# Pixel-major rows of the deformable-convolution stage by DMA transposes in a ring of four, and a reordered head

## The chip, the core and the metric

One core of one Trainium2 chip. The metric is the device time of one execution in microseconds (us), lower is better. TensorE writes only to PSUM; ScalarE (ACT), VectorE (DVE) and GpSimd (POOL) do the elementwise work; SyncE (SP) issues every DMA of this kernel, and the core's 16 DMA engines carry them out.

## What is computed

Two layers on `x` of shape (4, 128, 64, 64), f32. The first is group norm, a 1x1 convolution to q, k, v, attention over all 4096 pixels of an image, a projection and a residual. The second is the part that the change touches:

```python
out = relu(batchnorm(conv2d(x, w1), g1, b1))                 # h1
offsets = conv2d(out, w_off) + b_off                         # 18 channels
out = batchnorm(deform_conv(out, offsets, w2), g2, b2)       # samples h1 at 9 shifted points per pixel
return relu(out + x)

# deform_conv, in short
px = clip(row + tap_x + offset_x, 0, Hp - 1)                 # py likewise
xo = g_lt*xf[x0,y0] + g_rb*xf[x1,y1] + g_lb*xf[x0,y1] + g_rt*xf[x1,y0]
out = conv(xo, w, stride 3)
```

## The kernel before

Every f32 operand of a large matmul is split in two f16 halves, a high one and a low one, and a product is three matmuls (hi x hi, lo x hi, hi x lo). Engines run their own instruction streams, tied by semaphores: `after(engine, key, n)` waits until the n-th event of a kind; `stored(engine, sem, n)` waits for the n-th DMA on a semaphore. GpSimd first raises all semaphores by a constant (`OPEN`, L386 to L390) so that negative counts can be waited for, and the other engines wait for that (`s_open`).

Head (0 to 20 us). SyncE loads the first weights, the first image in four pieces (L272), the constants (L273) and the other weights (L274). VectorE scales the query weights, copies a product of weights from PSUM (L779) and makes the low halves of the weights (L783) once ScalarE has made the high ones (L559); then come the eight `gn_stats` of the image (L841), the group means over TensorE, and the affine of group norm on GpSimd (L401).

Then the attention of four images, which SyncE accompanies with 512 DMA transposes of probabilities (L290, 14 blocks of 128x128 f16 each), the first convolution of layer two, and its batch norm.

The offset stage (1699 to 1808 us) works on 32 bands of 8 image rows, 8 bands for each of 4 images. For band n: ScalarE makes h1 = relu(scale*y + bias) into one of four buffers `HT` (L699). TensorE turns it in four 128x128 pieces into PSUM (L1280). VectorE splits h1 into the padded halves `PDh`, `PDl` (L1024, L1026), which TensorE multiplies with the offset weights in 27 matmuls packed four to the array (L1290). The turned rows are pixel-major: ScalarE writes their high half (L656) and VectorE their low half (L1031) into `XS`, two buffers, and SyncE stores each band in four DMAs of 64 KB (L327) into the DRAM scratch `xt_dram`. The offsets themselves go from PSUM over `offset_rows` (L665), selection matmuls (L1298) and `offset_pixels` (L671) into `OFF`. The last image's stage also prepares the first hats on ScalarE (L679, L682). The order on ScalarE is: h1 of band n, rows of band n-2, offset rows of n-3, offset pixels of n-4. On VectorE it is: the split of band n, then the rows of band n-2.

After it, the sampling stage (1809 to 2323 us): SyncE loads windows of the stored rows (L345), queued behind all row stores; GpSimd makes interpolation weights (L524), TensorE turns them (L1311), samples (L1134 to L1136) and applies the second convolution.

The waits that order the offset stage on TensorE are few:

```python
after(pe, "hA", n + 1)            # h1 of this band
after(pe, "xe", n - 1)            # PSUM of the turned rows free
...                               # four pe.transpose, L1280
after(pe, "hp", b * NCH + min(rb + 2, NCH))
after(pe, "oe", n - 1)
...                               # 27 matmuls, L1290
```

## Time and profile before

| what | value |
|---|---|
| median of 3 runs | 2370.48 us (2368.9 to 2371.01) |
| the profiled execution's own time | 2370.24 us |
| its span | 2368.3 us |
| PE / DVE / ACT / POOL busy | 95% / 76% / 76% / 61% of the span |
| DMA queue q1 | 375.35 MB, 68.8% of 16 engines |
| mean granted TensorE clock | 0.984 |

The profile is one execution: its page gives busy shares, the span in 40 slices, the chain of work that ended last and the costliest groups; the trace behind it can be asked for single instructions. A wait is put down to the semaphore event that came last. In a timeline a row gives start, length, engine, line and operation, and in brackets the idle time ahead of it and what ended it.

### The profile page before, as it was taken

What the parts mean: (1) busy time and instruction counts of PE and PEld (TensorE: products, weight loads), DVE (VectorE), ACT (ScalarE), POOL (GpSimd) and SP (SyncE); (2) the same over time, 40 slices, a digit from 0 to 9 for tenths busy, and PEclk for the clock granted to TensorE, in tenths of its full rate; (3) what the DMA queues carried; (4) which work ended last, traced back from release to release, by engine and by line L of the source; (5) the groups of instructions that cost most, each with busy time, mean ns of one, the idle gap of its engine ahead of it and who ended that gap; (6) DMA issues with size and microseconds to landing.
All of it is one profiled execution on the core that took longest, in us unless ns stands there. A gap on an engine that the chain in (4) does not pass through costs nothing.

```text
span 2368.3 us, 73191 instructions
## 1 busy us (share of the span) xinstructions
PE 2260.2 (95%) x26668; PEld 1823.8 (77%) x26668; DVE 1808.2 (76%) x3885; ACT 1801.6 (76%) x2968; POOL 1448.9 (61%) x1103
## 2 busy tenths in 40 slices
PE   5999999999999999999999999969898999999994
PEld 3677777777777777777777777758666999999994
DVE  6778877777877777887777777758676887887887
ACT  5788888888888888888888888823376777776776
POOL 4569656666655666665666666675224666666661
PEclk9999999999999999999999999989999999999997
DMA  3878888879998888898787777786034444333447
GB/s 93 190 173 167 177 181 161 176 179 169 180 187 150 179 176 171 179 165 154 167 178 176 175 175 176 178 248 203 16 82 125 140 121 128 113 121 104 131 127 289
DMA packets 1048760, 377.63 MB, mean 159 GB/s; under 512 B 975490, under 2 KB 1035523, under 8 KB 1040387
## 3 DMA queue, kind: packets, MB, share of 16 engines
q1 hardware_dynamic: 1048578, 375.35, 68.8%
q8 instruction: 97, 1.59, 0.3%
q14 instruction: 85, 0.69, 0.1%
HBM read 98.69 MB, written 41.68 MB: 59 GB/s over the span
## 4 chain that ended last, share of the span: by engine, by line
PE 53%; POOL 24%; issue 16%; DVE 4%; DMA 2%; ACT 1%; POOLq 1%; SPq 0%; DVEq 0%; ACTq 0%
POOL interp L524 12%; POOL probs_split L416 10%; PE psum L1134 9%; PE psum L1135 9%; PE psum L1136 9%; PE psum L1174 7%; PE psum L1176 7%; PE psum L1175 7%; PE psum L1290 2%; DMA probsT_dma<-probs_split 2%; PE psum L1160 2%; PE psum L1298 1%; POOL col_hats L515 1%; POOL row_hats L510 1%; DVE neg_max L793 1%
## 5 line engine op out<-in xcount | busy, mean ns | idle before, releaser
L416 POOL TENSOR_TENSOR probs_split<-probs,probs_split 128x896 f16<-128x896 f32 x512 | 967.3, 1889 | 523.6 <-ACT probs_split L588 523.5
L793 DVE TENSOR_REDUCE neg_max<-psum 128x1 f32<-128x1024 f32 x512 | 626.4, 1223 | 307.6 <-PE psum L1136 305.3
L585 ACT ACTIVATE probs<-psum,exp_bias 128x1024 f32<-128x1024 f32 x512 | 570.5, 1114 | 184.6 <-DVE exp_bias L795 183.7
L1174 PE MATMUL psum<-vT_hi,probsT_dma 128*128 128x129 f16 x3584 | 637.6, 221 | 9.6 <-DMA probsT_dma<-probs_split 9.5
L1176 PE MATMUL psum<-vT_hi,probsT_dma 128*128 128x129 f16 x3584 | 637.3, 219 | 0.0
L1175 PE MATMUL psum<-vT_lo,probsT_dma 128*128 128x128 f16 x3584 | 637.1, 218 | 0.0
L588 ACT ACTIVATE probs_split<-probs 128x896 f16<-128x896 f32 x512 | 486.6, 950 | 23.1 <-ACT probs L585 1.0
L524 POOL TENSOR_TENSOR interp<-row_hats,col_hats 128x360 f32<-128x360 f32 x384 | 295.6, 798 | 185.4 <-PE psum L1311 174.4
L1134 PE MATMUL psum<-k_hi,q_hi 128*128 128x512 f16 x1024 | 388.5, 379 | 4.5 <-DVE q_lo L909 2.5
L1135 PE MATMUL psum<-k_lo,q_hi 128*128 128x512 f16 x1024 | 388.6, 379 | 0.0
L1136 PE MATMUL psum<-k_hi,q_lo 128*128 128x512 f16 x1024 | 388.6, 379 | 0.0
L1174 PEld LDWEIGHTS psum<-vT_hi,probsT_dma 128*128 128x128 f16 x3584 | 347.5, 97 | 11.2 <-DMA probsT_dma<-probs_split 10.9
L1175 PEld LDWEIGHTS psum<-vT_lo,probsT_dma 128*128 128x128 f16 x3584 | 352.8, 98 | 0.0
L1176 PEld LDWEIGHTS psum<-vT_hi,probsT_dma 128*128 128x128 f16 x3584 | 345.0, 96 | 0.0
L730 ACT ACTIVATE sampled_hi<-psum 128x432 f16<-128x432 f32 (+1 forms) x384 | 181.3, 497 | 81.3 <-PE psum L1136 81.2
L1063 DVE TENSOR_TENSOR sampled_lo<-psum,sampled_hi 128x432 f16<-128x432 f32 (+1 forms) x384 | 206.3, 554 | 47.1 <-ACT sampled_hi L730 42.5
L1055 DVE TENSOR_TENSOR interpT_lo<-psum,interpT_hi 120x384 f16<-120x384 f32 x384 | 190.4, 551 | 48.4 <-ACT interpT_hi L721 47.7
L1134 PE MATMUL psum<-sampled_hi,weights_hi 128*128 128x128 f16 x1152 | 214.4, 220 | 0.6 <-DVE sampled_lo L1063 0.6
L1136 PE MATMUL psum<-sampled_hi,weights_lo 128*128 128x128 f16 x1152 | 213.0, 219 | 0.0
L1135 PE MATMUL psum<-sampled_lo,weights_hi 128*128 128x128 f16 x1152 | 212.7, 219 | 0.0
L1134 PE MATMUL psum<-interpT_hi,xt_windows 120*128 120x144 f16 x1024 | 208.6, 227 | 2.1 <-DMA xt_windows<-xt_scratch 1.8
L721 ACT ACTIVATE interpT_hi<-psum 120x384 f16<-120x384 f32 x384 | 161.2, 492 | 64.9 <-PE psum L1311 54.2
(189 smaller groups left out, 4912.6 us busy)
## 6 DMA issues: line engine op xcount, KB each, us to landing
xt_windows<-xt_scratch SPq DMA_DIRECT2D x192, 320.0 KB
xt_scratch<-zeros_f SPq DMA_DIRECT2D x28, 576.0 KB, 4.3
probsT_dma<-probs_split SPq DMA_TRANSPOSE x512, 3.5
x_residual<-x SPq DMA_DIRECT2D x128, 64.0 KB, 2.4
x_scratch<-x_out SPq DMA_DIRECT2D x128, 64.0 KB, 2.1
x_rows<-x_scratch SPq DMA_DIRECT2D x32, 256.0 KB, 3.4
xt_scratch<-xt_stage SPq DMA_DIRECT2D x128, 64.0 KB
x_image<-x SPq DMA_DIRECT2D x3, 2048.0 KB, 9.1
```

Of the source, the lines that this page charges most:

```text
L416: po.tensor_tensor(PH[j][:, 1, :], P[:, j, 0:128 * DT[j]], PH[j][:, 0, :], ALU.subtract).then_inc(s["pl"], 1)
L524: last = po.tensor_tensor(SS[:, g % 2, :, WR * TW * a:WR * TW * a + WR * TW].rearrange("p k (j x) -> p k j x", j=WR), HX[:, hb, g, :, :, N ...
L585: act.activation(P[:, j, :], sc, ACT.Exp, bias=NB[:, par, j:j + 1]).then_inc(s["exp"], 1)
L588: act.activation(PH[j][:, 0, :], P[:, j, 0:128 * DT[j]], ACT.Copy).then_inc(s["ph"], 1)
L793: ve.tensor_reduce(NM[:, par, j:j + 1], sc, AX.X, ALU.max, negate=True).then_inc(s["mx"], 1)
L1063: ve.tensor_tensor(lo, src, hi, ALU.subtract).then_inc(s["xl"], 1)
L1134: pe.matmul(dst, lh, rh, start=start, stop=False)
L1135: pe.matmul(dst, lh, rl, start=False, stop=False)
L1136: return pe.matmul(dst, ll, rh, start=False, stop=stop)
L1174: pe.matmul(dst, th, Vh[:, p, v, 0:129], start=n == 0, stop=False)
L1175: pe.matmul(dst[:, 0:128], th, Vl[:, p, v, :], start=False, stop=False)
L1176: last = pe.matmul(dst, tl, Vh[:, p, v, 0:129], start=False, stop=n == KT - 1)
```

## The change

In the offset stage the four turns per band on TensorE, and the PSUM banks they filled, go. ScalarE and VectorE read h1 from `HT` in SBUF with a stride and write its two f16 halves, still channel-major, into a new ring `XI` of four buffers (in the space of weights no longer needed). SyncE issues one DMA transpose per band, of eight 128x128 blocks, from `XI` to `XS`, which now has four buffers as well; then the four stores of the band before it, which wait for that band's transpose. ScalarE's wait for `xt_stage` space becomes a wait for the transpose four bands back; the waits on the turns (`xt`) become waits on the low half (`xe`).

In the head the constants are loaded ahead of the image's third piece; ScalarE, VectorE and TensorE no longer wait for `s_open`; two small memsets on GpSimd come ahead of its semaphore increments; and the work on the weights moves on VectorE from ahead of the group-norm statistics into their waits.

```diff
+XBUF = 4
-        XS = sb_in(l1, "xt_stage", [128, 2, 4, 2 * C], F16)
+        XS = sb_in(l1, "xt_stage", [128, XBUF, 4, 2 * C], F16)
+        XI = WF[:, W_A:W_A + XBUF * TW * 128].bitcast(F16).rearrange("p (n r e i) -> p n r e i", n=XBUF, r=TW, e=2)
...
             for i in range(4):
+                if i == 2:
+                    sp.dma_start(CN[:, :], consts[:, 0:K_LO]).then_inc(s_k, 16)
                 sp.dma_start(XIN[:, 1024 * i:1024 * i + 1024], x[0, :, 1024 * i:1024 * i + 1024]).then_inc(s_xq[i], 16)
-            sp.dma_start(CN[:, :], consts[:, 0:K_LO]).then_inc(s_k, 16)
...
-            for b in range(B):
-                for rb in range(NCH):
-                    after(sp, "xe", b * NCH + (rb + 1))
-                    for r in range(TW):
-                        ...
-                        sp.dma_start(dst, XS[:, rb % 2, r, :]).then_inc(s_xs[rb % 2], 16)
+            def xt_store(m):
+
+                b, rb = divmod(m, NCH)
+                stored(sp, s_xi[rb % XBUF], m // XBUF + 1)
+                for r in range(TW):
+                    ...
+                    sp.dma_start(dst, XS[:, rb % XBUF, r, :]).then_inc(s_xs[rb % XBUF], 16)
+
+            for m in range(B * NCH):
+                after(sp, "xe", m + 1)
+                stored(sp, s_xs[m % XBUF], (m // XBUF) * TW)
+                sp.dma_start_transpose(XS[:, m % XBUF, :, :].rearrange("p r (e c) -> p (r e) c", e=2),
+                                       XI[:, m % XBUF, :, :, :].rearrange("p r e i -> p (r e i)")).then_inc(s_xi[m % XBUF], 16)
+                if m:
+                    xt_store(m - 1)
+            xt_store(B * NCH - 1)
...
-            after(po, "xt", B * NCH)
+            after(po, "xe", B * NCH)
...
-            act.wait_ge(s_open, 1)
...
-            def h1_staged(m, par):
-                after(act, "xt", m + 1)
-                act.wait_ge(s_xs[par], (m - par) * 32 + OPEN)
-                src = PS[:, 4 + par, :].rearrange("p (t c) -> p t c", c=C)
-                act.activation(XS[:, par, :, 0:C], src, ACT.Copy).then_inc(s["xth"], 1)
+            def h1_staged(m, at):
+                after(act, "hA", m + 1)
+                act.wait_ge(s_xi[at], (m - at) * (16 // XBUF) + OPEN)
+                src = HT[:, at, :].rearrange("p (i r) -> p r i", r=TW)
+                act.activation(XI[:, at, :, 0, :], src, ACT.Copy).then_inc(s["xth"], 1)
...
-                        after(act, "xt", n - 3)
+                        after(act, "xe", n - 3)
...
-                        h1_staged(n - 2, rb % 2)
+                        h1_staged(n - 2, (rb + 2) % 4)
...
-            ve.wait_ge(s_open, 1)
             ve.wait_ge(s_w, 16)
             link(ve.tensor_scalar(WF[:, 0:C], WF[:, 0:C], float(C) ** -0.5, None, ALU.mult))
-            ve.wait_ge(s_bp, 2)
-            link(ve.tensor_copy(WF[:, 2 * C:3 * C], PS[:, 6, 0:C]))
-            link(ve.tensor_scalar(SM[:, 2:3], vec(V_BQ), float(C) ** -0.5, None, ALU.mult))
-            ve.wait_ge(s_wh, 1)
-            link(ve.tensor_tensor(WL[:, 0:H_2], WF[:, 0:H_2], WH[:, 0:H_2], ALU.subtract))
-            ve.tensor_tensor(SM[:, 3:4], PS[:, 7, 0:1], vec(V_BP), ALU.add).then_inc(s_ws, 1)
-            ve.wait_ge(s_ws, 1)
...
             gn_channel(0)
+            ve.wait_ge(s_bp, 2)
+            link(ve.tensor_copy(WF[:, 2 * C:3 * C], PS[:, 6, 0:C]))
+            link(ve.tensor_scalar(SM[:, 2:3], vec(V_BQ), float(C) ** -0.5, None, ALU.mult))
             gn_group(0, 0)
+            ve.wait_ge(s_wh, 1)
+            link(ve.tensor_tensor(WL[:, 0:H_2], WF[:, 0:H_2], WH[:, 0:H_2], ALU.subtract))
+            ve.tensor_tensor(SM[:, 3:4], PS[:, 7, 0:1], vec(V_BP), ALU.add).then_inc(s_ws, 1)
+            ve.wait_ge(s_ws, 1)
             gn_affine(0)
...
-                        src = PS[:, 4 + rb % 2, :].rearrange("p (t c) -> p t c", c=C)
-                        xs = XS[:, rb % 2, :, :]
-                        ve.tensor_tensor(xs[:, :, C:2 * C], src, xs[:, :, 0:C], ALU.subtract).then_inc(s["xe"], 1)
+                        src = HT[:, (rb + 2) % 4, :].rearrange("p (i r) -> p r i", r=TW)
+                        xi = XI[:, (rb + 2) % 4, :, :, :]
+                        ve.tensor_tensor(xi[:, :, 1, :], src, xi[:, :, 0, :], ALU.subtract).then_inc(s["xe"], 1)
...
-            pe.wait_ge(s_open, 1)
...
-                        after(pe, "hA", n + 1)
-                        after(pe, "xe", n - 1)
-                        for r in range(TW):
-                            src = HT[:, rb % 4, :].rearrange("p (i r) -> p r i", r=TW)[:, r, :]
-                            last = pe.transpose(PS[:, 4 + rb % 2, 128 * r:128 * r + 128], src, ident)
-                        last.then_inc(s["xt"], 1)
                         after(pe, "hp", b * NCH + min(rb + 2, NCH))
```

## Rows read from the trace of the kernel before

**Rows 1.** Timeline of TensorE, one band: start us, us, engine, line, operation.

```profile
1750.77 0.39 PE L1290 MATMUL psum<-padded_hi,offset_w 128*32 128x512 f16 x2
...
1752.41 1.07 PE L1298 MATMUL psum<-late_constants,offset_rows 128*128 128x18 f32 x8
1753.33 0.70 PE L1280 MATMUL psum<-constants,h_rows 128*128 128x128 f32 x4
1753.96 0.39 PE L1290 MATMUL psum<-padded_hi,offset_w 128*32 128x512 f16 x2
```

**Rows 2.** Busy by stretch: length, PE, PEld, DVE, ACT, POOL, clock, DMA share, GB/s.

```profile
1300.00:1322.00 22.00, 22.00 (x247) 16.57 (x245) 15.72 (x39) 18.43 (x29) 15.11 (x8) 1.00 0.78 179
...
1736.00:1762.00 26.00, 26.00 (x324) 16.66 (x316) 20.94 (x29) 18.15 (x41) 8.46 (x14) 1.00 0.32 81
...
1788.00:1810.00 22.00, 18.95 (x219) 13.03 (x219) 12.69 (x19) 15.26 (x34) 3.65 (x6) 0.98 0.32 82
```

**Rows 3.** Instructions by line, offset stage: duration ns min/median/max, first and last start us.

```profile
L699 ACT ACTIVATE h_rows<-y_then_z,small x32: 801/816/839, 1699.1 to 1796.2; 128x512 f32<-128x512 f32 x16, 128x512 f32 x16
L656 ACT ACTIVATE xt_stage<-psum x32: 576/597/598, 1701.3 to 1803.9; 128x512 f16<-128x512 f32 x32
L665 ACT ACTIVATE offset_rows<-psum,weights_f x64: 462/474/482, 1707.6 to 1806.2; 128x256 f32<-128x256 f32 x64
L1024 DVE CAST padded_hi<-h_rows x32: 421/748/833, 1700.0 to 1797.7; 128x512 f16<-128x512 f32 x32
L1026 DVE TENSOR_TENSOR padded_lo<-h_rows,padded_hi x32: 695/698/1289, 1700.8 to 1798.1; 128x512 f16<-128x512 f32 x32
L1031 DVE TENSOR_TENSOR xt_stage<-psum,xt_stage x32: 677/684/693, 1704.1 to 1804.5; 128x512 f16<-128x512 f32 x32
```

**Rows 4.** Timeline of SyncE's queue, single row stores of one band.

```profile
1754.14 0.59 SPq L327 DMA_DIRECT2D xt_scratch<-xt_stage  x1
1754.77 0.60 SPq L327 DMA_DIRECT2D xt_scratch<-xt_stage  x1
```

**Rows 5.** End of the stage: SyncE's queue, TensorE's first sample, window loads by line.

```profile
1807.28 0.59 SPq L327 DMA_DIRECT2D xt_scratch<-xt_stage  x1
...
1809.74 0.34 SPq L345 DMA_DIRECT2D xt_windows<-xt_scratch  x1
...
1817.90 0.22 PE L1134 MATMUL psum<-interpT_hi,xt_windows 120*128 120x144 f16 x1 [1.80 <-DMA xt_windows<-xt_scratch]
...
L345 SPq DMA_DIRECT2D xt_windows<-xt_scratch x192: 286/287/342, 1809.7 to 2305.2; - x192
```

**Rows 6.** The costliest of ScalarE's hats steps, by line.

```profile
L679 ACT ACTIVATE col_hats<-col_hats,small x9: 1730/1747/1747, 1785.9 to 2314.0; 128x1728 f32<-128x1728 f32 x9
```

**Rows 7.** DMA transposes of the attention, by line: time on SyncE, then time to landing.

```profile
L290 SPq DMA_TRANSPOSE probsT_dma<-probs_split x512: 1294/1477/7261, 50.0 to 1542.7; - x171
...
DMA to landing us min/median/max: 3.4/3.5/10.4
```

**Rows 8.** Start of the stage: busy by stretch, and the first row store.

```profile
1703.00:1706.00 3.00, 3.00 (x27) 0.86 (x27) 2.75 (x5) 0.00 (x0) 0.14 (x1) 0.50 0.02 5
...
1704.85 0.80 SPq L327 DMA_DIRECT2D xt_scratch<-xt_stage  x1
```

**Rows 9.** The head: loads with landing times, statistics, table load, first affine.

```profile
L272 SPq DMA_DIRECT2D x_image<-x x4: 420/432/432, 1.2 to 2.6; - x4
...
DMA to landing us min/median/max: 4.3/6.7/7.9
...
constants<-consts SPq DMA_DIRECT2D x1, 227.0 KB, 8.1
...
8.64 1.28 ACT L559 ACT_TABLE_LOAD   x1 [8.64 <-DVE weights_f L779]
11.35 4.84 DVE L841 BATCH_NORM_STATS2 gn_stats<-x_image 128x6 f32<-128x512 f32 x8
19.65 7.44 POOL L401 TENSOR_SCALAR x_image<-x_image,small 128x512 f32<-128x512 f32 x8 [0.69 <-DVE small L881]
```

More of the change, by code:

```diff
@@ L190, in build @@
         ss = SS[:, :, :, :].rearrange("p a k w -> p (a k w)")
-        FX = [WF[:, W_A:W_A + PIECE], WF[:, W_A + PIECE:W_A + 2 * PIECE], wg[:, 0:2 * PIECE].bitcast(F32), xs.bitcast(F32), XT[:, :], XM[:, :]]
+        FX = [WF[:, W_A:W_A + PIECE], WF[:, W_A + PIECE:W_A + 2 * PIECE], wg[:, 0:2 * PIECE].bitcast(F32), xs[:, 0:2 * PIECE].bitcast(F32), XT[:, :], XM[:, :]]
         for k in range(NBUF - 1):
@@ L220, in build @@
         s_xc = [sem(f"rows_loaded{i}") for i in range(4)]
-        s_xs = [sem(f"xt_stored{i}") for i in range(2)]
+        s_xs = [sem(f"xt_stored{i}") for i in range(XBUF)]
+        s_xi = [sem(f"xt_dma_transposed{i}") for i in range(XBUF)]
         s_ld = [sem(f"windows_loaded{i}") for i in range(NBUF)]
@@ L237, in build @@
             hA="h1_ready", hp="h1_split", of="offset_conv", oe="offset_rows_ready", ot="offset_transposed",
-            ocp="offset_copied", xt="h1_transposed", xth="h1T_hi_ready", xe="h1T_ready",
+            ocp="offset_copied", xth="h1T_hi_ready", xe="h1T_ready",
             hd="distances", hb="distances_abs", hx="hats_ready", pr="interp_ready", fin="offset_steps", sh="pass_shift",
@@ L320, in _ @@
             sp.wait_ge(s_zf, 16 * 28)
-            for b in range(B):
-                for rb in range(NCH):
-                    after(sp, "xe", b * NCH + (rb + 1))
-                    for r in range(TW):
-                        slot = (b * IMG_ROWS + (GUARD + 8 * rb)) * PITCH + (1 + r * SLOTS)
-                        dst = bass.AP(xt_dram.tensor, slot * (2 * C), [[PITCH * 2 * C, 8], [2 * C, WW // TW], [1, 2 * C]])
-                        sp.dma_start(dst, XS[:, rb % 2, r, :]).then_inc(s_xs[rb % 2], 16)
+            def xt_store(m):
+                b, rb = divmod(m, NCH)
+                stored(sp, s_xi[rb % XBUF], m // XBUF + 1)
+                for r in range(TW):
+                    slot = (b * IMG_ROWS + (GUARD + 8 * rb)) * PITCH + (1 + r * SLOTS)
+                    dst = bass.AP(xt_dram.tensor, slot * (2 * C), [[PITCH * 2 * C, 8], [2 * C, WW // TW], [1, 2 * C]])
+                    sp.dma_start(dst, XS[:, rb % XBUF, r, :]).then_inc(s_xs[rb % XBUF], 16)
[7 more added lines that the diff above has]
+            xt_store(B * NCH - 1)
             ry, rx = sp.alloc_register("passes_y"), sp.alloc_register("passes_x")
@@ L347, in image_windows @@
                     def image_windows(b, last):
-                        for i in range(2):
-                            stored(sp, s_xs[i], b * (NCH * 2) + NCH * 2)
+                        for i in range(XBUF):
+                            stored(sp, s_xs[i], b * (NCH // XBUF * TW) + NCH // XBUF * TW)
                             sp.sem_inc(s_go, 1)
@@ L352, in image_windows @@
                             if i == HH // TW - 1 and not last:
-                                stored(sp, s_xs[0], b * (NCH * 2) + (NCH * 2 + TW))
+                                stored(sp, s_xs[0], b * (NCH // XBUF * TW) + (NCH // XBUF * TW + TW))
                                 sp.sem_inc(s_go, 1)
@@ L385, in _ @@
         def _(po):
+            po.memset(SM[:, 0:1], -0.5).then_inc(s_pz, 1)
+            po.memset(SM[:, 1:2], 1.0).then_inc(s_pz, 1)
             for k in s:
                 po.sem_inc(s[k], OPEN)
-            for k in s_xo + s_xs + s_tr:
+            for k in s_xo + s_xs + s_tr + s_xi:
                 po.sem_inc(k, OPEN)
@@ L391, in _ @@
             po.memset(OW[:, :, :, :], 0.0).then_inc(s_pz, 1)
-            po.memset(SM[:, 0:1], -0.5).then_inc(s_pz, 1)
-            po.memset(SM[:, 1:2], 1.0).then_inc(s_pz, 1)
             po.memset(Vh[:, :, :, 128:129], 1.0).then_inc(s_pz, 1)
@@ L1141, in _ @@
             pe.matmul(PS[:, 6, 0:C], WF[:, 2 * C:3 * C], WF[:, W_PROJ:W_PROJ + C], start=True, stop=True).then_inc(s_bp, 1)
-            pe.wait_ge(s_ws, 1)
             pe.wait_ge(s_k, 16)
@@ L1234, in _ @@
             group_means(0, 0)
+            pe.wait_ge(s_ws, 1)
             after(pe, "gn", 4)
```

## The prediction, made before the changed kernel was run

> **What bounds the kernel now.** I read the page first: no stretch has TensorE idle for long, so a stage must be read by its own rhythm and by what ends last in it. The change touches two places: the head (the first 20 us) and the offset stage, which runs from 1699 us to 1808 us. It works on 32 bands, eight for each of four images. The timeline of TensorE gives the rhythm of a band in the steady stretch: the 27 matmuls of the offset convolution start at 1750.77, the selection matmuls at 1752.41, the four turns of h1 (L1280) at 1753.33, and the next band's convolution at 1753.96, so 1.64 + 0.92 + 0.63 = 3.19 us, back to back [rows 1]. TensorE is the bound there: 26.00 us busy of 26.00 at clock 1.00, with the DMA engines a third busy [rows 2]. ScalarE has in each band 0.82 (h1) + 0.60 (high half of the rows) + 2 x 0.47 (offset rows), 2.4 us with a small copy of the offset pixels on top, for which I take 0.2 more [rows 3]. VectorE has 0.75 + 0.70 + 0.68 = 2.13 us, and its subtraction L1026 takes up to 1.29 us in some bands [rows 3].
>
> The queue that decides is SyncE's. Its single instructions show row stores of 0.60 us at a pitch of 0.64 us (1754.14, 1754.77), and a band has four, so 2.56 us [rows 4]. SyncE is thus taken for 2.56 of 3.19 us, 80%. That 0.60 us is SyncE's own time, not the DMA engines': these are only 0.32 busy [rows 2].
>
> The stage ends thus: last store issued at 1807.28, done 1807.87; first window load issued 1809.74; first sampling matmul at 1817.90, after 1.80 us of waiting for just those windows [rows 5]. So the path that sets the end of this stage is SyncE's last store. TensorE's own work ahead of it was done by 1816.1.
>
> **The change, part by part.** *Turns removed from TensorE:* 0.63 us in each band; TensorE then needs 1.64 + 0.92 = 2.56 us [rows 1]. This is a saving only if nothing else is slower than 3.19 us.
>
> *ScalarE and VectorE read h1 from SBUF with a stride and write the halves into the ring.* ScalarE: between 0.60 us as now from PSUM and 0.82 us, the 512-wide L699 from SBUF, so 0 to +0.22 us [rows 3]. VectorE: the nearest row is L1026, 0.70 us (0.68 now) and at worst 1.29 us, so at worst 0.75 + 1.29 + 1.29 = 3.3 us for a band [rows 3]. Both stay under the queue computed below, so I cost them at nothing. Without that cover ScalarE's 2.6 us and in image 3 four hats steps of at most 1.75 us, 7.0 us over eight bands, would make 3.5 us per band there at most [rows 6].
>
> *A DMA transpose of eight 128x128 blocks is added on SyncE for each band.* It stands ahead of the stores of the band before, and these wait for the landing of that band's transpose. Queued behind it: the four stores, the next transpose, and after the last band all window loads. Its issue time T is the unknown. The row there is: the transpose of 14 blocks holds SyncE for 1.477 us in the middle and 1.294 at least [rows 7]. In proportion to blocks T is 0.74 from the least and 0.84 from the middle one; with the 0.60 us of a store as a fixed part, T = 0.60 + 8/14 x (1.48 - 0.60) = 1.10; if blocks cost nothing, 1.29. I take 1.0, between 0.84 and 1.10, because every issue in the trace has some fixed part. SyncE's band is then 2.56 + 1.0 + 0.04 (the gap behind an instruction, as between stores) = 3.60 us, more than the 3.19 of today and far more than TensorE's 2.56. **SyncE becomes the bound**; from 3.34 (T 0.74) to 3.89 (T 1.29).
>
> The Trainium skill, VectorE: DVE Perf Modes, Rules for kernel authors, speaks against the change in general: it says to turn 128x128 on TensorE if PSUM will do and by DMA otherwise. By the rows four turns cost TensorE 0.63 us [rows 1] and a transpose of 14 blocks 1.48 us on SyncE [rows 7]; following the rule, the sum would be the head's -2.7 us alone.
>
> *Working of the end.* The first transpose starts where the first store did, 1704.85: the first row subtraction on VectorE stands behind three bands of splitting in both versions [rows 8]. The landing of a larger transpose takes 3.5 us [rows 7], so the first stores run from 1708.35 to 1710.91. Then come 30 times (transpose + four stores) and four last stores: 1710.91 + 30 x 3.60 + 2.56 = 1821.5, against 1807.87, or **+13.6 us**. In general the shift is 30 P - 94.4 us for a band of P. Later landings are covered: a transpose has P + T = 4.6 us before its stores are due. The DMA engines have room: in 22 us with eight 14-block transposes they were 0.78 busy, 17.2 us, some 2.05 us each once the small loads and stores are taken off; 8/14 of it is 1.2 us, with 1.0 us of stores now (0.32 x 3.19), 2.2 of 3.60 us [rows 2]. The rings of four let ScalarE, VectorE and TensorE run ahead by up to four bands, which moves their own end to about where it is (1807 to 1808) but not SyncE's.
>
> *After the stage.* The windows come 13.6 us later and the first sampling matmul with them. TensorE has only two tiles to turn meanwhile, so it stands idle for over 12 us. After its idle time ahead of the offset stage the granted clock is 0.50 for the first 3 us of matmuls [rows 8], 1.2 GHz of the two levels, so 3 us hold 1.5 us of work: I add **+1.5 us** (0 to 1.5). No gain from the longer wait: before, GpSimd had also been two tiles ahead.
>
> *The head.* Three engines no longer wait for GpSimd's semaphore increments (6.9 us), and VectorE's weight work moves behind the statistics. Now the statistics start at 11.35, behind the chain product - copy - table load (8.64, 1.28 us) - split, and take 4.84 us [rows 9]. Image pieces land between 1.2 + 4.3 = 5.5 and 2.6 + 7.9 = 10.5 us [rows 9]. The constants, issued 0.43 us behind the last piece, go ahead of the last two now; they landed at 3.0 + 8.1 = 11.1, so the last piece now lands at about 11.2, and the statistics of its two chunks (4.84/8 each) end at 12.4 instead of 16.2. But the table load now waits for the copy, which sits behind the channel step: copy at 13.5, ScalarE done at 15.4, split and bias until 16.2, then the affine steps (0.6 us): GpSimd starts at 16.95 instead of 19.65 [rows 9]: **-2.7 us** (-3.5 to -1.7). All behind it moves along. The GpSimd memsets moved ahead of the increments are 0.1 us each, on nobody's path.
>
> *Sum:* the profiled execution has 2370.24 us for its span of 2368.3, and the median of the runs is 2370.48, so it stands for them. 2370.24 + 13.6 + 1.5 - 2.7 = **2382.6 us**. Its own range: 5.8 + 1.5 - 3.5 = +3.8, 2374.0, to 22.3 + 1.5 - 1.7 = +22.1, 2392.3.
>
> **The rivals.** *A: the issue is cheap (faster).* SyncE issues a window load, a bigger transfer, in 0.287 us [rows 5]. If a transpose of eight blocks cost T = 0.29, P would be 2.89 and the shift 30 x 2.89 - 94.4 = -7.7 us. ScalarE's band in image 3 gives about 1.7 of this back, so 2370.24 - 6.0 - 2.7 = 2361.5. It decides from T below 0.48 (30 P - 94.4 - 2.7 under -4.7 needs P < 3.08, with no cold start). Against it: no transpose in the trace was issued in under 1.29 us [rows 7]. The Trainium skill, DMA: Bandwidth & Descriptors, Issuing engines are not separate DMA queues, calls the sequencer's time to start a DMA "usually small relative to the DMA itself", which would make this case. The trace disagrees for the stores: 0.60 us of issue against 0.32 x 3.19 / 4 = 0.26 us of DMA work. Chance 0.18.
>
> *B: the issue costs as much as a store's (no change).* T = 0.60, P = 3.20, shift +1.6, hardly any cold start (+0.5): 2370.24 + 1.6 + 0.5 - 2.7 = 2369.6. The TensorE saving is eaten exactly by the queue. Chance 0.12.
>
> *C: the clock falls (much slower).* TensorE would work 2.56 of 3.60 us. If the grant went to 0.50 for it, the convolution's 1.64 us would be 3.3 us and the selection's 0.92 would be 0.92 to 1.8, a band of 4.2 to 5.1, say 4.5: 32 x (4.5 - 3.19) = +42, about 2410. For: the row of the cold start. Against: at 18.95 us busy of 22 the clock was 0.98 [rows 2]. Chance 0.06. Late landings of the transposes (up to 10.4 us seen [rows 7]), a few us more per image, 0.04.
>
> **How the numbers follow.** Forecast 0.60, A 0.18, B 0.12, C and late landings 0.10. The range 2366 to 2393 holds the forecast with its bounds, B, and the issue times between A and B, and leaves out A itself and C. A measurement of this kernel tells about 0.2%, 4.7 us, from no change: faster 0.18, same 0.14 (B and a little of the forecast's lower end), slower 0.68. The likeliest case's own range is 2374 to 2392.
>
> **What would show it.** Right: SyncE's queue without a gap from the first transpose to the last store, a band of 3.3 to 3.9 us, a transpose of eight blocks held for 0.8 to 1.3 us; no L1280; TensorE with idle time in each band, ended by ScalarE or VectorE, these by the landing of a transpose; the first window load at about 1809.74 + 13.6 - 2.7 = 1820.6; the statistics of the head ending near 12.4 and GpSimd's first affine near 17. Wrong: an issue under 0.6 us; a last store earlier than today's; ScalarE or VectorE busy without gaps; a granted clock well under 1.00 through the stage.

## The result and the profile after

The changed kernel takes 2397.07 us (median of 4 runs, 2395.54 to 2398.92) against 2370.4 us for the kernel before on the same chip: ratio 1.0118, 95% interval 1.0107 to 1.013, some 27 us slower. The profiled execution took 2398.92 us with a span of 2397.0, 28.7 us above the span of before; its mean granted clock is 0.974.

The page of after, its span and the chain that ended last:

```profile
span 2397.0 us, 72973 instructions
PE 50%; POOL 23%; issue 16%; SPq 3%; DVE 3%; DMA 2%; ACT 1%; POOLq 1%; DVEq 0%; ACTq 0%
```

The new thing is "SPq 3%" in the chain: SyncE's queue, not on it before (0%), is on it for some 3% of 2397 us. The timeline of that queue at the start of the offset stage, in its middle and at its end (start us, us, engine, line, operation, count; the queue is written SPq):

```profile
1702.24 3.23 SPq L337 DMA_TRANSPOSE xt_stage<-weights_f  x2
1705.51 3.89 SPq L332 DMA_DIRECT2D xt_scratch<-xt_stage  x4
...
1750.09 1.23 SPq L337 DMA_TRANSPOSE xt_stage<-weights_f  x1
1751.37 2.53 SPq L332 DMA_DIRECT2D xt_scratch<-xt_stage  x4
1754.00 1.23 SPq L337 DMA_TRANSPOSE xt_stage<-weights_f  x1
...
1826.06 5.10 SPq L332 DMA_DIRECT2D xt_scratch<-xt_stage  x8
1832.80 1.35 SPq L359 DMA_DIRECT2D xt_windows<-xt_scratch  x3
```

From 1750.09 to 1754.00 is one band: 1.23 + 2.53 us of issuing and 0.05 + 0.10 us of gaps, 3.91 us, where [rows 1] has 3.19. The durations by line (ns, min/median/max), what SyncE waited for within the stage (us, times, longest), and TensorE's first sample:

```profile
L337 SPq DMA_TRANSPOSE xt_stage<-weights_f x32: 1231/1232/2232, 1702.2 to 1824.8; - x32
L332 SPq DMA_DIRECT2D xt_scratch<-xt_stage x128: 596/603/1035, 1705.5 to 1830.6; - x128
...
SPq L337 <- DVE weights_f L1043: 2.5, 3, 0.9
...
1841.02 0.28 PE L1146 MATMUL psum<-interpT_hi,xt_windows 120*128 120x144 f16 x1 [16.52 <-DMA xt_windows<-xt_scratch]
```

The queue waits 2.5 us in 130. The last store ends at 1831.16 instead of 1807.87, the first window load starts at 1832.80 instead of 1809.74, the first sample at 1841.02 instead of 1817.90 [rows 5]: 23.1 us late, although the stage began earlier (below). The other engines have time left. The middle of the stage (length, PE, PEld, DVE, ACT, POOL, clock, DMA share, GB/s), and the copies of ScalarE and VectorE with what ScalarE waited for:

```profile
1736.00:1762.00 26.00, 21.75 (x245) 12.77 (x237) 19.67 (x23) 17.54 (x32) 8.51 (x12) 0.87 0.63 135
...
L669 ACT ACTIVATE weights_f<-h_rows x32: 1106/1136/1252, 1698.4 to 1812.3; 128x512 f16<-128x512 f32 x32
L1043 DVE TENSOR_TENSOR weights_f<-h_rows,weights_f x32: 1054/1075/1249, 1701.1 to 1813.5; 128x512 f16<-128x512 f32 x32
...
ACT weights_f L669 <- DMA xt_stage<-weights_f: 17.5, 18, 1.9
```

TensorE is busy 21.75 us of 26 where it was busy all 26 [rows 2]; ScalarE waits for the transpose four bands back, that is for SyncE's queue to come round. After the stage TensorE starts cold, that is at the lower granted clock. First the changed kernel, then the kernel before in a stretch of the same stage:

```profile
1842.00:1846.00 4.00, 4.00 (x29) 3.93 (x27) 2.05 (x4) 2.34 (x5) 0.00 (x0) 0.50 0.62 195
```

```profile
1826.00:1830.00 4.00, 4.00 (x64) 3.99 (x61) 3.26 (x9) 2.69 (x6) 4.00 (x4) 1.00 0.62 178
```

At a granted clock of 0.50 these 4 us hold 29 matmuls, at 1.00 they hold 64. ScalarE's large hats steps (128x1728, part of making the interpolation weights) mark the progress of the sampling stage. The first of them in the changed kernel, then the first and the last in the kernel before:

```profile
1883.10 1.75 ACT L692 ACTIVATE col_hats<-col_hats,small 128x1728 f32<-128x1728 f32 x1
```

```profile
1857.17 1.75 ACT L679 ACTIVATE col_hats<-col_hats,small 128x1728 f32<-128x1728 f32 x1
...
2322.05 1.66 ACT L682 ACTIVATE col_hats<-col_hats 128x1728 f32<-128x1728 f32 x1
```

The first is 25.9 us late, and comes 42.1 us behind the first sample where it was 39.3: the cold start costs 2.8 us. Other runs bear out that the clock is the reason. In the two executions of the kernel with the new head alone (below), the granted clock in the first 4 us of sampling was 0.64 and 0.86 and the distance 40.6 and 39.8 us, between the 42.1 at 0.50 and the 39.3 at 1.00. The head (table load, last statistics, first affine):

```profile
0.76 1.28 ACT L572 ACT_TABLE_LOAD   x1 [0.76 <-PEq L1455]
11.09 1.29 DVE L846 BATCH_NORM_STATS2 gn_stats<-x_image 128x6 f32<-128x512 f32 x2 [0.59 <-DMA x_image<-x]
16.14 7.41 POOL L415 TENSOR_SCALAR x_image<-x_image,small 128x512 f32<-128x512 f32 x8 [0.76 <-DVE small L886]
```

The affine starts 3.5 us earlier than in [rows 9]. The last row that matters is the end: ScalarE's last large hats step, and a wait of TensorE behind it for which the trace shows no releaser:

```profile
2345.98 1.66 ACT L695 ACTIVATE col_hats<-col_hats 128x1728 f32<-128x1728 f32 x1
...
PE psum L1148 <- issue: 3.7, 1, 3.7
```

In the kernel before that step starts at 2322.05, as shown above. From it to the end of the span are 46.25 us before and 51.02 now. So the 28.7 us are 25.9 at the first hats step (the head's gain already in it), -2.0 between it and the last one (both kernels have two slow steps there, of 60.1 and 60.5 us before, 58.5 and 60.1 now), and +4.8 in the tail.

### The profile page after: what moved, and what is told of

It reads as the page before. It is cut to its first block, busy times and chain, and to the rows that moved or that the text cites. A ratio compares the mean times of both kernels' runs of the same rounds, so it can differ in the third digit from the quotient of the medians.

```text
span 2397.0 us, 72973 instructions
## 1 busy us (share of the span) xinstructions
PE 2256.4 (94%) x26540; PEld 1817.9 (76%) x26540; DVE 1821.1 (76%) x3885; ACT 1815.4 (76%) x2968; POOL 1448.8 (60%) x1103
## 4 chain that ended last, share of the span: by engine, by line
PE 50%; POOL 23%; issue 16%; SPq 3%; DVE 3%; DMA 2%; ACT 1%; POOLq 1%; DVEq 0%; ACTq 0%
POOL interp L538 12%; POOL probs_split L430 10%; PE psum L1146 9%; PE psum L1147 9%; PE psum L1148 9%; PE psum L1184 7%; PE psum L1186 7%; PE psum L1185 7%; SPq L332 2%; DMA probsT_dma<-probs_split 2%; PE psum L1170 2%; SPq L337 1%; POOL col_hats L529 1%; POOL row_hats L524 1%; DVE neg_max L798 1%
## 5 line engine op out<-in xcount | busy, mean ns | idle before, releaser
L1146 PE MATMUL psum<-interpT_hi,xt_windows 120*128 120x144 f16 x1024 | 209.4, 228 | 17.0 <-DMA xt_windows<-xt_scratch 16.5
L1148 PE MATMUL psum<-interpT_hi,xt_windows 120*128 120x144 f16 x1024 | 208.4, 227 | 3.7 <-issue 3.7
```

What stands on the lines that cost most here:

```text
L1146: pe.matmul(dst, lh, rh, start=start, stop=False)
L1148: return pe.matmul(dst, ll, rh, start=False, stop=stop)
```

## The experiments

**Theory Q (queue):** SyncE's issue time is the whole loss; TensorE's saving is worth nothing because another engine needs as long. **Rival R (chain):** the loss is in the new waits, transpose landing to store, ring to ScalarE. **Rival D:** the DMA engines or the strided copies are slower. All ratios are to the kernel before.

**Head alone**, in the kernel before (the head's edits as in the diff of the change, nothing of the offset stage):

> The kernel before with the reordered head alone. Theory (the head gives 3.5 us, the offset stage costs the rest): first affine of GpSimd at about 16.1 us instead of 19.65, time 2370.4 - 3.5 = about 2367. Rival (the gain is taken back in the attention, which is paced by other things): 2370 within 0.5 us though the affine starts early.

2364.77 us (10 runs), ratio 0.9979 (0.9969 to 0.9988). Its first window load:

```profile
1805.40 2.47 SPq L346 DMA_DIRECT2D xt_windows<-xt_scratch  x5
```

That is 4.3 us before the one of [rows 5]. The gain is small, so the same kernel was timed a second time:

> The kernel before with the reordered head alone, timed in five rounds: the best version so far. Theory: its first affine is 3.5 us earlier and nothing takes it back: ratio to before 0.9985 or below (2366.5 or less), with an interval that leaves out 1.

2366.16 us (12 runs) against 2368.49 (17 runs), ratio 0.9986 (0.9976 to 0.9996). Both intervals lie below 1: a gain of 3 to 5 us. It is the fastest version found whose output is right.

**Offset stage alone** (the changed kernel with the head of before):

> The changed kernel with the head of before. Theory: the offset stage costs 23 us at SyncE's last store, 2 to 3 us more for a cold TensorE in sampling, and some for the end of the run: 2397 + 3.5 = about 2400.5. Rival (the two parts act on each other, say by code loading): off by more than 2 us from the sum of both parts.

2402.24 us, ratio 1.0135 (1.0118 to 1.0152).

```profile
1834.71 5.20 SPq L358 DMA_DIRECT2D xt_windows<-xt_scratch  x10
```

The windows come as late as in the changed kernel, and a transpose takes the same 1.232 us. The stage costs 32 us by this ratio; with the head's 3 to 5 us off, the two parts add up to the 27 of both within their intervals.

**One transpose added to the kernel before.** This isolates the queue: TensorE still turns, ScalarE and VectorE still read PSUM, the rings stay two, and nobody on the other engines waits for the added transpose.

```diff
+        XD = sb_in(l1, "extra_turned", [128, 2, 8, 128], F16)
...
                     after(sp, "xe", m + 1)
+                    if m >= 2:
+                        stored(sp, s_xi[m % 2], m // 2)
+                    sp.dma_start_transpose(XD[:, m % 2, :, :], WH[:, 0:1024]).then_inc(s_xi[m % 2], 16)
```

> The kernel before, TensorE's turns and both rings of two kept, with one DMA transpose of eight blocks per band added on SyncE into a buffer that nobody reads. Theory (SyncE's issue time is the whole loss): SyncE without gaps at about 1.23 + 0.05 + 2.56 = 3.9 us per band, last store about 1829, time about 2370.4 + 22 + 2 = 2394. Rival (the loss is in the strided reads, the landing ahead of the stores or the ring): SyncE is late by less than half of that, time under 2382.

2395.23 us, ratio 1.0113 (1.0094 to 1.0133), +25 us. Its queue, its first window loads and its middle stretch:

```profile
1817.30 1.24 SPq L329 DMA_TRANSPOSE extra_turned<-weights_hi  x1
1818.59 2.54 SPq L333 DMA_DIRECT2D xt_scratch<-xt_stage  x4
1821.23 1.23 SPq L329 DMA_TRANSPOSE extra_turned<-weights_hi  x1
...
1835.03 5.20 SPq L353 DMA_DIRECT2D xt_windows<-xt_scratch  x10
...
1736.00:1762.00 26.00, 21.80 (x249) 13.78 (x251) 16.04 (x22) 15.32 (x35) 4.09 (x7) 0.93 0.62 129
```

A band is 1817.30 to 1821.23, 3.93 us, and the first window load comes at 1835.03, as with the offset stage alone (1834.71). R falls for the stage, and so does the part of D on the strided copies: with none of the change's waits on the other engines, and ScalarE and VectorE reading PSUM as before, the whole delay of the windows is there. The part of D on the DMA engines isn't settled by this run, since the added transpose loads them as well (0.62 busy); the next run settles it. This run also shows that behind such a queue taking the turns off TensorE gains nothing, since this kernel still has them. But it is 6.7 us shorter in span than the offset stage alone, all of it behind the windows: 5.0 in the tail (46.3 against 51.3 us, from the last hats step to the end) and 2.7 in the two slow steps, with 1.0 lost ahead of these. What the tail hangs on is the subject of the last experiment.

**The row stores issued by GpSimd**, four bands behind, so that SyncE has only the transposes:

```diff
+            def xt_store(m):
+                stored(po, s_xi[rb % XBUF], m // XBUF + 1)
+                    po.dma_start(dst, XS[:, rb % XBUF, r, :]).then_inc(s_xs[rb % XBUF], 16)
             for m in range(B * NCH):
+                if m >= 4:
+                    xt_store(m - 4)
                 after(po, "hA", m + 1)
```

> The changed kernel with the four row stores of a band issued by GpSimd, so that SyncE issues transposes alone. Theory (SyncE is the bound, next is ScalarE with 0.82 + 1.14 + 0.83 + 0.23 = 3.0 us): if GpSimd issues a store in under 0.7 us the band is about 3.1 us and the time 2364 to 2369. If GpSimd needs over 1 us for a store, it is the bound: four stores and a memset, 4.6 us or more per band, and the time is over 2400. Rival (SyncE's issue is not what holds the stage): the time stays at 2397 within 4 us with SyncE idle for over half of the stage.

2372.69 us (10 runs), ratio 1.0005 (0.9994 to 1.0016): 24 us of the 27 are back, though some 4 us of what was expected are missing. GpSimd in the stage and at its end:

```profile
L509 POOL DMA_DIRECT2D xt_scratch<-xt_stage x128: 597/597/807, 1704.2 to 1813.6; - x128
...
1809.50 4.72 POOL L509 DMA_DIRECT2D xt_scratch<-xt_stage  x8 [3.49 <-DMA xt_stage<-weights_f]
1814.23 8.51 POOL L536 TENSOR_TENSOR interp<-row_hats,col_hats 128x360 f32<-128x360 f32 x11
```

The issue costs 0.597 us on GpSimd too; there it is paid beside SyncE. The DMA engines and the strided copies do the same work as in the changed kernel, so D falls and Q is confirmed for the stage. The tail is still 50.9 us, 4.7 above the kernel before. What is last next is GpSimd: its last stores end at 1814.2 and its interpolation weights stand behind them. The Trainium skill, DMA: Bandwidth & Descriptors, Issuing engines are not separate DMA queues, has it that issuing from several engines saves only the sequencer's time; the trace agrees, 0.60 us on either engine, and adds that here this time was nearly all of the stage's loss.

**Stores split, two on SyncE and two on GpSimd:**

```diff
-                for r in range(TW):
+                for r in range(2):                       # SyncE
...
+                for r in range(2, TW):                   # GpSimd, three bands behind
+                    po.dma_start(dst, XS[:, rb % XBUF, r, :]).then_inc(s_xp[rb % XBUF], 16)
```

> The changed kernel with two of a band's four row stores on SyncE and two on GpSimd, which issues one in 0.60 us too. SyncE has 1.28 + 1.28 + 0.1 = 2.66 us, GpSimd 1.2 + 0.55 = 1.8, so ScalarE's 3.0 us (0.82 + 1.14 + 0.83 + 0.23) are the bound: band 3.05, last store at about 1702 + 32 x 3.05 + 5 = 1805, time 2361 to 2366. If it stays above 2370, something other than the three queues holds the stage.

2372.84 us (10 runs), ratio 1.0008 (0.9997 to 1.0019). This missed its expectation by 7 us at the least. SyncE is no longer full, and what it waits for is VectorE, VectorE behind ScalarE's copy; ScalarE's groups from 1710 to 1800 us (busy us, mean ns, idle before):

```profile
SPq L339 <- DVE weights_f L1059: 17.3, 15, 3.3
...
L685 ACT ACTIVATE weights_f<-h_rows 128x512 f16<-128x512 f32 x28 | 32.9, 1175 | 0.0
L694 ACT ACTIVATE offset_rows<-psum,weights_f 128x256 f32<-128x256 f32 x56 | 23.1, 468 | 0.0
L728 ACT ACTIVATE h_rows<-y_then_z,small 128x512 f32 (+1 forms) x25 | 20.3, 813 | 0.6 <-DVE weights_f L1059 0.5
L700 ACT ACTIVATE offsets<-psum 128x72 f32 (+1 forms) x27 | 6.2, 228 | 9.6 <-PE psum L1319 9.5
```

ScalarE stands still 10.2 us of 90; a band of it is 1.17 + 0.83 + 0.81 + 0.23 = 3.04 us (the two offset rows overlap: 23.1 us for 28 bands), and hats come on top. With the queue relieved, ScalarE with its longer copy takes nearly the 3.19 us that TensorE took before. The next experiment, without transposes, helps to sort the miss. There too ScalarE is busy for 82.2 us of the 90, but the DMA engines only 0.32 against 0.79 here, so they don't set that pace. From ScalarE's last copy to the first window load are 11.1 us here (1798.1 to 1809.2) and 7.2 there (1796.7 to 1803.9): here the last transposes must land before their stores. The copies themselves run from first to last in 104.5 us against 98.8; why is not shown. And the tail is 51.0 us, 4.7 above the kernel before.

**The turning left out** (no transposes; the stores read the channel-major halves, so the rows in DRAM aren't turned and the output is wrong): the change at its best price.

```diff
-                sp.dma_start_transpose(XS[:, m % XBUF, :, :]..., XI[:, m % XBUF, :, :, :]...)
-                if m:
-                    xt_store(m - 1)
-            xt_store(B * NCH - 1)
+                xt_store(m)
```

> The changed kernel without its DMA transposes: SyncE stores the channel-major halves from their ring as they are, so the pixel-major rows that sampling reads are wrong. Theory (issue time alone): SyncE has 2.56 us per band again and ScalarE's 3.0 us set the pace; last store at about 1702 + 32 x 3.05 = 1800, time about 2362 to 2366. Rival (strided reads or rings hold the stage): over 2380.

2367.99 us (10 runs), ratio 0.9985 (0.9976 to 0.9995). SyncE waits again, for VectorE:

```profile
SPq L331 <- DVE weights_f L1038: 14.6, 21, 3.7
```

It was expected at 2362 to 2366. With turning for nothing on every engine the kernel is still no faster than the reordered head alone (2364.8 to 2366.2). But its tail is 51.8 us instead of 46.3. Without these 5.5 us it would take 2362.5 us, an estimate, 2 to 4 us less than the head alone: that is the most that removing the turns could be worth here.

**How the issue time depends on the size.** Two transposes of four blocks per band, and one of sixteen per two bands:

```diff
-                sp.dma_start_transpose(XS[:, m % XBUF, :, :]..., XI[:, m % XBUF, :, :, :]...)
+                for r0 in (0, 2):
+                    sp.dma_start_transpose(XS[:, m % XBUF, r0:r0 + 2, :]..., XI[:, m % XBUF, r0:r0 + 2, :, :]...)
```

> The changed kernel with two DMA transposes of four blocks per band in place of one of eight. It measures the issue time by block count. If it is proportional to blocks (0.15 us a block), the band stays at 3.9 us and the time at 2397. If most of it is a fixed part (from 1.23 us for 8 blocks and 1.48 for 14: 0.9 fixed, 0.04 a block), a transpose of four takes 1.07, the band is 3.9 + 0.95 = 4.85 us and the time 2397 + 30 = 2427.

```diff
+                after(sp, "xe", m + 2)
+                sp.dma_start_transpose(XS[:, m % XBUF:m % XBUF + 2, :, :]..., XI[:, m % XBUF:m % XBUF + 2, :, :, :]...)
```

> The changed kernel with one DMA transpose of 16 blocks for two bands. With a fixed part of 0.9 us and 0.04 a block it takes 1.56 us, the band on SyncE is 2.56 + 0.8 = 3.4 us, and the time 2397 - 16 = about 2381. If the time is proportional to blocks, 2.46 us each and no change, 2397. Rival (two pairs are too few buffers, ScalarE and SyncE wait for each other): over 2400.

2435.2 us (ratio 1.027, 1.025 to 1.0291) and 2419.14 us (ratio 1.0199, 1.0182 to 1.0216). The transposes of the first, then of the second, then the second's queue and wait:

```profile
L338 SPq DMA_TRANSPOSE xt_stage<-weights_f x64: 1188/1251/1823, 1699.1 to 1860.1; - x64
```

```profile
L339 SPq DMA_TRANSPOSE xt_stage<-weights_f x16: 1707/1881/2005, 1703.5 to 1839.2; - x16
...
1731.26 5.56 SPq L332 DMA_DIRECT2D xt_scratch<-xt_stage  x8
1738.54 1.71 SPq L339 DMA_TRANSPOSE xt_stage<-weights_f  x1
...
1747.69 2.00 SPq L339 DMA_TRANSPOSE xt_stage<-weights_f  x1
...
SPq L254 <- DMA xt_scratch<-xt_stage: 23.0, 14, 1.8
```

Four blocks cost 1.25 us, eight 1.23, fourteen 1.48 (1.29 at least, in the attention, where the DMA engines are busier) [rows 7], sixteen 1.88: up to eight blocks the price is one fixed sum. The expectations had taken 0.9 us as the fixed part and were too low. Sixteen are cheaper per block, but the second kernel lost by what its expectation named as the rival, too few buffers: the queue stands still from 1736.8 to 1738.5: with two pairs of buffers the next transpose waits until the stores of two pairs back have landed. A band is then 9.15 / 2 = 4.57 us.

**A ring of two in place of four** in the changed kernel:

```diff
-XBUF = 4
+XBUF = 2
```

> The changed kernel with rings of two in place of four for halves and staging. Theory (SyncE's queue is the bound, more buffers only let the others run ahead): with two, the chain from one transpose over its landing (3.1 us), the two halves (1.14 + 1.08) and the next issue closes every second band, about 7 us per two bands, still under 2 x 3.9 = 7.8, so the time is 2397 within 4 us. Rival (the ring of four hides landings): a band of over 4.2 us, over 2407.

2445.1 us, ratio 1.0317 (1.0297 to 1.0337): 48 us slower than the change. My expectation, that only the queue counts, was wrong.

```profile
L337 SPq DMA_TRANSPOSE xt_stage<-weights_f x32: 1231/1232/2361, 1697.7 to 1870.4; - x32
SPq L254 <- DMA xt_scratch<-xt_stage: 49.7, 30, 1.8
```

The issues are unchanged; the 49.7 us in 30 waits for landings of stores are the difference. The rings of four hide these entirely: in the changed kernel SyncE waits in this stage only the 2.5 us for VectorE.

**ScalarE's copy relieved**, in the kernel with split stores. First the order turned round: read h1 as it lies, write with a stride.

```diff
-                src = HT[:, at, :].rearrange("p (i r) -> p r i", r=TW)
-                act.activation(XI[:, at, :, 0, :], src, ACT.Copy).then_inc(s["xth"], 1)
+                src = HT[:, at, :].rearrange("p (i r) -> p i r", r=TW)
+                act.activation(XI[:, at, :, 0, :].rearrange("p r i -> p i r"), src, ACT.Copy).then_inc(s["xth"], 1)
... (VectorE's subtraction in the same order)
```

> The split stores with ScalarE and VectorE walking h1 in memory order and writing the halves with a stride, the same values. It measures what the stride on the f32 read costs: the copy on ScalarE takes 1.14 us with it, 0.61 us is the unstrided row of the attention's head. If the read stride is the cost, ScalarE needs 2.5 us per band, TensorE's 2.56 becomes the bound and the time falls by 32 x 0.45 = 14 at most, to 2360. If the strided f16 write costs as much or more, 2373 or above.

Then, with the order as it was, the same copy made by GpSimd in place of ScalarE:

```diff
+                po.tensor_scalar(XI[:, m % XBUF, :, 0, :], HT[:, m % 4, :].rearrange("p (i r) -> p r i", r=TW), 1.0, None, ALU.mult).then_inc(s["xth"], 1)
```

> The split stores with the high half of the rows made by GpSimd from h1. ScalarE has 1.9 us per band, GpSimd 0.8 to 1.2 + 1.2 + 0.55 = 2.6 to 3.0 us, and in image 2 1.0 to 1.3 us more. Theory (ScalarE's 3.05 us bound the split version): band 2.7 to 3.0 us, time 2373 - 5 to 10 = 2363 to 2368. If GpSimd is the bound or holds VectorE up, 2373 or more.

2403.85 us (ratio 1.0144, 1.0125 to 1.0162) and 2401.8 us (ratio 1.0139, 1.0116 to 1.0161). The copies, of the first and of the second:

```profile
L685 ACT ACTIVATE weights_f<-h_rows x32: 2462/2528/2674, 1696.8 to 1822.6; 128x512 f16<-128x512 f32 x32
L1059 DVE TENSOR_TENSOR weights_f<-h_rows,weights_f x32: 2433/2470/3441, 1699.4 to 1825.1; 128x512 f16<-128x512 f32 x32
```

```profile
L532 POOL TENSOR_SCALAR weights_f<-h_rows x32: 1982/2134/2809, 1694.1 to 1823.9; 128x512 f16<-128x512 f32 x32
```

Both are dearer than the strided read of 1.17 us, and in the second GpSimd itself is the bound, busy for 89.5 us of the 90 from 1710 to 1800. That ScalarE's copy is the one next bound behind the queue is thus argued from the rows of the split stores, not shown by a kernel in which it was cheaper.

**The tail.** The ten kernels without the turns on TensorE have a tail of 50.9 to 51.8 us with a wait for "issue" of 3.4 to 3.9 us; the four with them have 46.3 and no such wait. (Within each group TensorE's code of these stages is the same, so this is one observation repeated.) Theory L: TensorE's instructions of the last tile lie elsewhere in its stream once the 64 turns in front of them (16 bands in the code, of which eight are looped) are gone. Rival: something else in the change makes the wait. First the turns kept in their place, on a constant, with nobody reading them:

```diff
+                        after(pe, "hA", n + 1)
+                        for r in range(TW):
+                            pe.transpose(PS[:, 4 + rb % 2, 128 * r:128 * r + 128], ident, ident)
                         after(pe, "hp", b * NCH + min(rb + 2, NCH))
```

> The changed kernel, with four unneeded turns of a constant per band on TensorE in the place of the removed ones; nobody reads them. From the start of the last hats step to the end the changed kernel takes 51.0 us and the kernel before 46.3. Theory L (the stall in the last tile goes with the place of its instructions in TensorE's stream, which the 64 removed turns have moved): the stall of 3.7 us goes, the tail is 46.3 us, and the total falls by about 4.8 us, to 2392. Rival (something else in the change causes it): tail 51.0, total 2397. TensorE's 0.63 us more per band costs nothing in both, since SyncE's 3.91 us stay the bound; were the removal of the turns worth anything, the first window load would be later than 1832.8.

Then 64 turns, and 96, in one piece ahead of the wait for the first windows:

```diff
+                            if first and g == 1 and i == 0:
+                                for k in range(64):           # 96 in the second
+                                    pe.transpose(PS[:, 7, 0:128], ident, ident)
```

> The changed kernel, with 64 unneeded turns of a constant in one piece ahead of TensorE's wait for the first windows, where it stands idle for 16.5 us. At 0.16 us each they take some 10 us of it, so about 6 us of idle time stay. Theory L (place in the stream): the last tile's code lies where it lay before, the tail is 46.3 us instead of 51.0, about -4.8 us. Rival: 51.0. Clock: if 6 us of idle time are short enough, the first sample runs at a granted clock near 1.00 and the first hats step of the sampling stage comes 2.8 us earlier, 1880.3 instead of 1883.1; if not, as before. Total 2389.5 with both, 2392 with L alone, 2397 with neither.

> As the run with 64 turns, with 96: they take some 15 us, so TensorE works until about the first sample. Clock theory: granted clock near 1.00 from the first sample on, first hats step at about 1880.3 instead of 1883.1. Theory L: the last tile's instructions lie 32 turns further on than in the kernel before, at a place that no run has tried, so the tail may be 46.3 or 51; the rival of L has 51.0. If clock theory is wrong the first hats step stays at 1883.1 or comes later.

2390.65 us (ratio 1.0101, 1.0084 to 1.0118) and 2390.78 us (1.0093, 1.0071 to 1.0116); a single 2393.51 us with 96. The last hats step in spans of 2386.8, 2388.7 and 2391.4 us, of the third also TensorE's wait behind it:

```profile
2340.47 1.66 ACT L695 ACTIVATE col_hats<-col_hats 128x1728 f32<-128x1728 f32 x1
```

```profile
2342.39 1.66 ACT L695 ACTIVATE col_hats<-col_hats 128x1728 f32<-128x1728 f32 x1
...
1838.57 0.28 PE L1146 MATMUL psum<-interpT_hi,xt_windows 120*128 120x144 f16 x1 [9.03 <-DMA xt_windows<-xt_scratch]
...
1836.00:1840.00 4.00, 1.43 (x13) 1.46 (x14) 0.00 (x0) 0.07 (x1) 0.00 (x0) 0.50 0.64 156
```

```profile
2343.62 1.66 ACT L695 ACTIVATE col_hats<-col_hats 128x1728 f32<-128x1728 f32 x1
...
PE psum L1147 <- issue: 1.3, 1, 1.3
```

The tails are 46.3, 46.3 and 47.8 us. With 64 turns added, whether at the old place or elsewhere, the stall is gone; with 32 turns more it is there again with 1.3 us, in one execution. L stands as far as three placements go: 4.8 us of the change's loss hang on where TensorE's instructions lie and not on what the change does. By what mechanism the place costs time is not shown. The totals' intervals alone would not have shown it (1.0101 against 1.0118); the tail in the trace does. Of the 10.2 us between the spans of the changed kernel and of the first of these, 4.7 are the tail and 3.4 an earlier start of the stage (first transpose at 1698.79 instead of 1702.24).

That first kernel also repeats the test of TensorE's saving: its queue needs 129.9 us from the first transpose to the first window load, the changed kernel 130.6, so the turns cost nothing there. The clock part of the expectation was not put to the test: the turns took 0.11 to 0.12 us each, so TensorE still stood idle for 9.0 and 6.0 us, and the clock was 0.50 at the first sample. From there to the first hats step are 41.6 and 41.1 us against 42.1 in the changed kernel and 39.3 before, so about a third of the cold price of 2.8 us was saved at best.

## Why the prediction was wrong in size and right in kind

**The bound: right.** SyncE's queue without gaps sets the stage, TensorE has idle time in each band, ScalarE waits for landings; the first window load waits behind the last store. The added transpose shows that the issue time alone is enough for it.

**T, the term that was mis-sized: the step that failed.** I took 1.0 us, a value from between a share of 8/14 and a store's 0.60 as the fixed part; it is 1.232 us, within the bounds of 0.74 and 1.29 that I gave and next to the upper one, the least time of the 14-block transpose [rows 7]. The transpose of four blocks shows why: nothing of the price goes away with the blocks. The row that I had was itself the better estimate; a scaling without a second size in the trace was a guess. The gaps of a band beyond the pitch of the stores are 0.12 us instead of 0.04 (the two added waits stand there), so P is 3.91 instead of 3.60.

T alone does not carry the result out of the range: with 1.23 in its place the sum would be 2389.6. Its 7.0 us, 5.4 us of gaps and slow issues in the same queue, and 4.8 us in the tail, for which the sum had no term at all, do it together.

**The working of the end: right, with the sizes put in.** The first stores end at 1709.40 us, where 1710.91 - 2.7 = 1708.2 was forecast: 1.2 late, since the first issues are slow (3.89 us for four stores). From there to the last four stores the queue takes 30 bands in 1831.16 - 2.55 - 1709.40 = 119.2 us, 3.97 each: 3.91 and some longer issues. 1.2 + 30 x 0.37 = 12.3 us is what the windows are later than forecast: 1832.80 against 1820.6. Of this T is 30 x 0.23 = 7.0, the gaps are 30 x 0.08 = 2.4, the longer issues 30 x 0.06 = 1.8, the first ones 1.2.

**Copies costed at nothing: right in the sum, wrong in size.** ScalarE's strided copy took 1.14 us where 0.60 to 0.82 was the bound, VectorE's 1.075, within 0.70 to 1.29. Its worst band of ScalarE also had a slip: 2.6 + 0.9 = 3.5 us leaves out the 0.22 that the copy was allowed, so it should have been 3.7, more than the 3.60 of the queue that was to cover it. Measured, ScalarE's band is 3.0 us, 3.9 with those hats, the length of the queue's 3.91: the cover held, but only because the queue came out longer as well. It spoils every repair: together with the tail of 4.7 to 5.5 us it is the nearest reason that the rows give why no kernel with a relieved queue gets below the head alone. The Trainium skill, SBUF — State Buffer, Door 1: The DMA port swizzle, says in its note on lines of 16 bytes that each access which crosses to a new line pays; h1 is read here at steps of 16 bytes. The trace agrees in sign, 1.14 us against 0.60 for as many elements from PSUM [rows 3] and 0.61 from SBUF in one piece (the attention's `h_hi<-x_image`), but the page gives four f32 as the stride that is still free, and by the measurement that stride is not.

**After the stage.** Cold clock: +2.8 instead of +1.5: the first 4 us were all at 0.50, and the following 4 at 0.89 on average. The share of DMA time was put at 2.2 of 3.60 us, 0.61; it is 0.63, but of 3.91 us, so 2.5 us. The tail's +4.8 us I had not thought of: I had costed the removed instructions at their time alone. The -2.0 between are within what two executions of one kernel show: the two slow steps of the head alone took 58.8 and 58.1 us in one, 59.2 and 60.5 in the other.

**The head.** Statistics ended at 12.4 as forecast; the affine started at 16.14, not 16.95: -3.5, the end of my range. I had left the table load behind VectorE's copy; it moved to 0.76 us when the wait for `s_open` went, though a wait for that copy still stands ahead of the activation in the code. At the batch norm ahead of the offset stage 2.8 us of it are left (1693.51 against 1696.30), but there the executions differ: with the same head it came at 1688.7 to 1693.5.

**The sum.** The forecast had +12.4 us. 12.2 (queue) + 1.3 (clock) - 2.0 (slow steps) + 4.8 (tail) = 16.3 more make the 28.7 measured in the span. The range ended at 2393 and 2397.07 was measured; its upper bound had T = 1.29, but no price for slow first issues, two more waits or a moved instruction stream.

**Rivals.** A (cheap issue) and B (a store's price) fall with T. The version that keeps the turns on TensorE is the fastest. The Trainium skill, VectorE: DVE Perf Modes, Rules for kernel authors, had that order for 128x128 blocks, and the runs agree with it. C: the granted clock did fall in the stage, to 0.87, though the row that I held against it had 0.98. TensorE had room for that, and SyncE's queue, which sets the stage, waited only 2.5 us in all. Late landings: ring waits of ScalarE only.

## What to carry to other kernels

Count the queue that issues DMAs as an engine: here a store costs 0.60 us of SyncE and a transpose of four or eight blocks 1.23 to 1.25, and a queue that is 80% full has no room for it. A saving on the bounding engine is worth at most the distance to the next one. Deeper rings hid landings (48 us between two and four buffers) but no issue time. Where an operation's cost has one row only, take that row as it stands unless a second size in the trace shows how it scales, and compare the tails of kernels before explaining the last few us by the work.

## What the runs showed of the hardware that I had not expected

- A DMA transpose from SBUF to SBUF holds SyncE's queue 1.25 us for 4 blocks, 1.23 for 8, 1.48 for 14 (least 1.29) and 1.88 for 16.
- The same store costs 0.60 us of issue on SyncE and on GpSimd.
- 512 elements per partition: a copy on ScalarE with f32 read at 16-byte steps takes 1.14 us, with f16 written at a step of 512 bytes 2.53 us; on VectorE 1.08 and 2.47; on GpSimd the strided read takes 2.13.
- The activation table load moved by 7.9 us (8.64 to 0.76) with the removal of one of the two waits ahead of the first activation.
- Removing 64 turns from TensorE's code put a wait of 3.7 us for nothing but "issue" into a tile 500 us later; adding 64 others, at either of two places ahead of it, took it out, adding 96 left 1.3 us (one execution).
